# Point-cloud window attention inside a Perceiver/Mamba layer: points of a sub-block 15 apart, centre loads on another queue, and layer 2 with value matmuls of its own

## The reference, cut to what matters

```python
neigh = gather(feats, inds)                                  # one window of 10 neighbours per point and order
gf = concatenate([broadcast(center), neigh - center], -1)    # 2*C channels, stacked over the 4 orders
x16 = x.astype(float16).astype(float32)                      # (B*N, 10, 256), heads of 32 channels
scores = einsum('bihd,bjhd->bhij', qh, qh) / sqrt(32)        # 10 x 10 per point and head
attn = softmax(scores)
fused = einsum('bhij,bjhd->bihd', attn, qh) @ W_lin.T        # 64 outputs, folded with W_conv
# then instance norm, leaky relu, and the maximum over the 10 neighbours
```

## Time and profile before

| | |
|---|---|
| median of 3 runs | 2704.42 us (2703.09 to 2705.81) |
| the profiled execution, its own time | 2693.29 us |
| its span, first to last instruction | 2691.5 us |
| mean granted clock of PE | 0.87 of full speed |
| PE busy, share of the span | 1997.2 us, 74% |
| DVE busy | 1852.2 us, 69% |
| ACT busy | 1381.4 us, 51% |
| POOL busy | 778.7 us, 29% |
| DMA | 263.01 MB in 494619 packets, 98 GB/s |
| a pair's window loads | QW 240 KB, QX 3 x 80 KB and 240 KB |

### The profile page before, as it was taken

One profiled execution on the slowest core, in us unless ns is written; L12 is line 12 of the kernel. 1 busy time (PEld: TensorE's weight loads), 2 busy tenths in 40 slices (PEclk: granted clock), 3 DMA queues, 4 the chain that ended last, 5 costly groups with the idle time before them and its releaser, 6 DMA issues. The chain is left out here.

```text
span 2691.5 us, 119989 instructions
## 1 busy us (share of the span) xinstructions
PE 1997.2 (74%) x48106; PEld 1420.5 (53%) x48106; DVE 1852.2 (69%) x4073; ACT 1381.4 (51%) x2858; POOL 778.7 (29%) x996
## 2 busy tenths in 40 slices
PE   0586636666666656648888888885789999999977
PEld 0124325556555634338888888883334544454432
DVE  7889975555555559964555555557758888888875
ACT  0489843333333359834555555554564555555532
POOL 0010023443444420033333333330024444444321
PEclk9996667777778765678999999997999999999988
DMA  1105665555555516654555554542022222222210
GB/s 51 12 6 133 150 152 113 130 127 127 129 128 129 126 43 151 149 128 109 115 111 115 115 115 112 117 105 80 25 86 78 90 77 79 82 82 78 82 55 18
DMA packets 494619, 263.01 MB, mean 98 GB/s; under 512 B 362667, under 2 KB 463947, under 8 KB 494408
## 3 DMA queue, kind: packets, MB, share of 16 engines
q1 hardware_dynamic: 489512, 257.92, 39.8%
q10 hardware_dynamic: 5024, 4.00, 0.6%
HBM read 208.85 MB, written 52.96 MB: 97 GB/s over the span
## 5 line engine op out<-in xcount | busy, mean ns | idle before, releaser
L872 PE MATMUL pQ<-QW,QX 128*30 128x42 f16 (+1 forms) x23040 | 709.3, 298 | 297.6 <-DMA QX<-scratch_q 264.0
L872 PEld LDWEIGHTS pQ<-QW,QX 128*30 128x30 f16 x23040 | 659.7, 142 | 323.9 <-issue 322.2
L981 POOL TENSOR_TENSOR Ap<-E,RM 128x450 f32<-128x450 f32 x384 | 371.9, 969 | 59.7 <-POOL RM L976 58.6
L1011 ACT ACTIVATE E<-Dm 128x150 f32<-128x150 f32 x384 | 125.9, 328 | 465.7 <-DVE Dm L938 465.5
L955 DVE TENSOR_REDUCE hmax<-Hs 128x450 f32 (+1 forms) x144 | 89.7, 623 | 325.1 <-ACT junk L1023 325.1
L976 POOL TENSOR_TENSOR RM<-R,own 128x45 f32<-128x45 f32 x384 | 100.5, 262 | 671.4 <-DVE R L944 671.0
L1016 ACT ACTIVATE Vs<-pQ 128x480 f32<-128x480 f32 (+1 forms) x384 | 292.5, 762 | 0.0
L928 DVE TENSOR_REDUCE mx<-pQ 128x15 f32<-128x150 f32 x384 | 116.4, 303 | 218.9 <-PE pQ L872 217.8
L949 DVE STREAM_TRANSPOSE AT<-Ap 128x480 f32<-128x480 f32 x384 | 244.6, 637 | 21.1 <-POOL Ap L981 19.6
L1969 POOL TENSOR_TENSOR MT<-cb,decay 128x512 f32 (+1 forms) x128 | 163.9, 1302 | 244.8 <-PEq L1737 147.9
L609 DVE TENSOR_TENSOR QT<-ext,cen 128x1650 f16<-128x1650 f32 x96 | 233.0, 2488 | 1.8 <-issue 1.5
(11 more groups left out here) (365 smaller groups left out, 3295.1 us busy)
## 6 DMA issues: line engine op xcount, KB each, us to landing
QW<-scratch_q SPq DMA_DIRECT2D x192, 240.0 KB, 3.0
QX<-scratch_q SPq DMA_DIRECT2D x576, 80.0 KB, 2.6
QX<-scratch_q SPq DMA_DIRECT2D x192, 240.0 KB, 3.4
scratch_q<-QT SPq DMA_DIRECT2D x120, 360.0 KB, 5.0
Wg<-in_in_proj SPq DMA_DIRECT2D x64, 256.0 KB, 2.7
Wh<-in_in_proj SPq DMA_DIRECT2D x64, 256.0 KB, 2.8
Wo<-in_out_proj SPq DMA_DIRECT2D x64, 256.0 KB, 2.6
W_s<-in_in_proj SPq DMA_DIRECT2D x16, 256.0 KB, 2.7
```

Source lines behind the costliest of these rows:

```text
L872: last = nc.tensor.matmul(pQ[32 * h:32 * h + PTS * K, p, u // PB, at0:at0 + ON], query, both, start=True, stop=True)
L981: nc.gpsimd.tensor_tensor(subs(A[:, p, :], 32)[:, :, 0:PTS * K].rearrange("p s (n j) -> p s n j", n=PTS), subs(E[:, p, :], K).unsqueeze(2) ...
```

## The change

- Sub-blocks: the three points of a sub-block are now 15 apart, so that sub-block is the fastest index of the points. The subtractions read both operands in sequence: three of 1800, 1800 and 1500 elements, one of 30, one of 60. The centre matmuls and the maximum over neighbours follow the new order.
- Centre loads: one tile CT without slots, loaded for CU sub-tiles at a time (4 in layer 1, 2 in layer 2). In layer 1 ACT issues them, behind the copy of the values; in layer 2 SP issues them four steps later than before.
- Layer 2: the matmul of keys and weights becomes two. Scores use 96 rows and 10 key columns, values 128 rows and the 64 weight columns from their own contiguous tile; the four score matmuls of a sub-block come first, then the four value matmuls. PSUM is split into pS and pV. The weights are no longer copied into QW.
- Layer 2: the mix uses one matmul with 64 stationary columns where there were two with 32.
- The rest of CT is zeroed on DVE, the pad sub-blocks of QT cover two runs more, and the second result tile is allocated after the second gathering.

```diff
@@ -605,18 +604,17 @@
-                    for n in range(PTS):
-                        v.tensor_tensor(QT[:, k, 0:LAST, n, :, 0:SUBS],
-                                        rows(ext, k, ahead + n, (GP, LAST), (1, K), (PTS, SUBS)),
-                                        rows(cen, k, n, (GP, LAST), (0, K), (PTS, SUBS)),
+                    runs_of = QT[:, k, :, :, :, :].rearrange("p g n j u -> p (g n) j u")
+                    for r0, r1 in zip(THIRDS, THIRDS[1:]):
+                        v.tensor_tensor(runs_of[:, r0:r1, :, 0:SUBS],
+                                        rows(ext, k, ahead + SUBS * r0, (SUBS, r1 - r0), (1, K), (1, SUBS)),
+                                        rows(cen, k, SUBS * r0, (SUBS, r1 - r0), (0, K), (1, SUBS)),
                                         ALU.subtract).then_inc(q_v, 1)
...
@@ -749,8 +749,8 @@
-        QW = sb("QW", [128, NU, UT * 4, ON * SW], F16)
-        CT = sb("CT", [128, NU, UT * GP], F16)
+        QW = sb("QW", [128, NU, UT * 4, (ON if WIDE else K) * SW], F16)
+        CT = sb("CT", [128, U * GP], F16)
...
-        pQ = ps("pQ", [128, 2, NB, 512])
+        if WIDE:
+            pQ = ps("pQ", [128, 2, NB, 512])
+        else:
+            pS, pV = ps("pS", [128, 2, 512]), ps("pV", [128, 2, 1024])
...
+        def load_centres(eng, at, k):
+
+            (t, r), w = at, k // CU
+            c16 = scratch["c16"].rearrange("p (v x) -> p v x", x=CU * GP)
+            eng.wait_ge(mixed, pack(r, k + CU - 1) + 1)
+            eng.dma_start(CT[0:2 * C, w * CU * GP:(w + 1) * CU * GP],
+                          c16[:, bass.ds(r * (U // CU) + w, 1), :].rearrange("p v x -> p (v x)")).then_inc(c_in[w], 16)
@@ -836,11 +854,8 @@
-                    if first:
-                        sp.wait_ge(ct_zeroed, 1)
-                    sp.wait_ge(mixed, pack(r, k + UT - 1) + 1)
-                    sp.dma_start(CT[0:2 * C, w, :], c16[:, bass.ds(r * NU + w, 1), :].rearrange("p v x -> p (v x)"))\
-                        .then_inc(c_in[w], 16)
+                if at(4) and (k - 4) % CU == 0 and not WIDE:
+                    load_centres(sp, at(4), (k - 4) % U)
@@ -850,27 +865,40 @@
...
                         for h in range(4):
-                            y = k % UT * 4 + h
-                            query = QX[:, w, y, :, :].rearrange("p n (j u) -> p u (n j)", u=SW)[:, u]
-                            both = QW[:, w, y, :].rearrange("p (x u) -> p u x", u=SW)[:, u]
-                            at0 = u % PB * ON
-                            last = nc.tensor.matmul(pQ[32 * h:32 * h + PTS * K, p, u // PB, at0:at0 + ON], query, both,
-                                                    start=True, stop=True)
+                            to = slice(32 * h, 32 * h + PTS * K)
+                            if WIDE:
+                                last = nc.tensor.matmul(pQ[to, p, u // PB, at0:at0 + ON], query[h], keys[h],
+                                                        start=True, stop=True)
+                            else:
+                                nc.tensor.matmul(pS[to, p, u * K:u * K + K], query[h][0:96], keys[h][0:96],
+                                                 start=True, stop=True)
+                        if not WIDE:
+                            for h in range(4):
+                                to = slice(32 * h, 32 * h + PTS * K)
+                                last = nc.tensor.matmul(pV[to, p, u * O:u * O + O], query[h], W["stack"][:, h, :],
+                                                        start=True, stop=True)
@@ -879,25 +907,24 @@
...
                     for u in range(SUBS):
-                        for slot, half in strips:
-                            at0 = slot * O + 32 * half
-                            last = nc.tensor.matmul(pH[at0:at0 + 32, p, 32 * u:32 * u + PTS * K],
-                                                    Vs[:, (first + slot) % RV, u * O + 32 * half:u * O + 32 * half + 32],
+                        for slot in range(SL):
+                            last = nc.tensor.matmul(pH[slot * O:slot * O + O, p, 32 * u:32 * u + PTS * K],
+                                                    Vs[:, (first + slot) % RV, u * O:u * O + O],
...
@@ -913,10 +940,11 @@
-            for k in range(1, U, 3):
+            for k in range(1, U if WIDE else 0, 3):
                 v.tensor_copy(*weights_of(k)).then_inc(placed[k // UT], 1)
+            v.memset(CT[2 * C:, :], 0.0).then_inc(ct_zeroed, 1)
@@ -952,8 +980,9 @@
-                    v.tensor_reduce(hmax[:, bass.ds(q * GP, GP)],
-                                    Hs[:, p, :].rearrange("p (n j) -> p n j", j=K), X, ALU.max).then_inc(hmax_done, 1)
+                    v.tensor_reduce(hmax[:, bass.ds(q * GP, GP)].rearrange("p (n s) -> p s n", n=PTS),
+                                    Hs[:, p, :].rearrange("p (s n j) -> p s n j", n=PTS, j=K), X, ALU.max)\
+                        .then_inc(hmax_done, 1)
@@ -1013,8 +1041,10 @@
...
+                if at(1) and (k - 1) % CU == 0 and WIDE:
+                    load_centres(act, at(1), (k - 1) % U)
```

More of the change, by code:

```diff
@@ L774, in window_attention @@
         q_in = [sem(f"q_in{k}") for k in range(NU)]
-        c_in = [sem(f"c_in{k}") for k in range(NU)]
+        c_in = [sem(f"c_in{k}") for k in range(U // CU)]
         projected = sem("projected")
@@ L852, in _ @@
             none = A[:, 0:2, :].rearrange("p k x -> p (k x)").bitcast(F16)
[L853 to L856, removed]
+            if WIDE:
+                cells = [pQ[:, p, b, :] for p in range(2) for b in range(NB)]
+                pe.wait_ge(rows_zeroed, 1)
+            else:
+                cells = [pS[:, p, :] for p in range(2)] + [pV[:, p, 512 * b:512 * b + 512] for p in range(2) for b in range(2)]
+            for cell in cells:
+                nc.tensor.matmul(cell, none[:, 0:128], none[:, 0:512], start=True, stop=True)
             def scores(k, at):
@@ L881, in mix @@
                     pe.wait_ge(copied, q + 1)
-                    for w in range(first // UT, k3 // UT + 1):
-                        pe.wait_ge(c_in[w], r * 16 + 16)
-                    strips = [(slot, half) for slot in range(SL) for half in range(O // 32)]
-                    for slot, half in strips:
-                        at0 = slot * O + 32 * half
[L888 to L893, removed]
+                    pe.wait_ge(c_in[first // CU], r * 16 + 16)
+                    if isinstance(t, int):
+                        pe.wait_ge(ct_zeroed, 1)
+                    for slot in range(SL):
+                        for half in range(O // 32):
+                            at0 = slot * O + 32 * half
+                            out = pH[at0:at0 + 32, p, 0:GC].rearrange("p (s x) -> p s x", x=32)[:, :, 0:PTS * K]\
+                                .rearrange("p s (n j) -> p s n j", n=PTS)
+                            ctr = CT[:, (first + slot) * GP:(first + slot + 1) * GP].rearrange("p (n s) -> p s n", n=PTS)\
+                                .unsqueeze(3).to_broadcast([128, SUBS, PTS, K])
+                            nc.tensor.matmul(out, W["center"][:, 32 * half:32 * half + 32], ctr, start=True, stop=False)
                     pe.wait_ge(vs_ready, t + 3)
@@ L990, in _ @@
             act.dma_start(own[:, :], io["own"]).then_inc(const_in, 16)
-            for k in range(0, U, 3):
+            for k in range(0, U if WIDE else 0, 3):
                 nc.scalar.activation(*weights_of(k), ACT.Copy).then_inc(placed[k // UT], 1)
```

56 lines of the change are left out of this document (33 added, 23 removed).

## The result

The changed kernel takes 3022.64 us (median of 4 runs, 3016.68 to 3027.27), the kernel before 2703.76 us beside it: a ratio of 1.1187, 95% interval 1.115 to 1.1223, 319 us slower where 316 us faster was forecast. The profiled execution spans 3025.5 us against 2691.5, at a mean granted clock of 0.725 against 0.87.

What follows compares the result with a forecast made beforehand. It took waits to hold the attention layers, window loads queued behind SP's centre load, and nearly full DVE and ACT the gather. Gains of 136 + 147 + 26 + 7 = 316 us took 2704.4 to 2388 us; range 2300 to 2545.

Steps and rivals of the forecast that it cites:

- Centre loads, layer 1: Layer 1: moving centre loads to ACT ends SP's queue stall; 11.70 to 8.8 us per pack, 136 us gained.
- rival 4: Layer 1: the centre wait isn't what holds it, its beat stays; 2524 us in total, chance 0.04.
- Rival 1: Layer 1: window transfers at 150 GB/s replace the stall; 9.7 us per pack, 2430 us in total, chance 0.08.
- Gathering: Gather stage: longer sequential subtractions shorten DVE until ACT takes over; 0.8 us per step, 26 us gained.
- Scores and values: Layer 2: sixty matmuls per sub-tile become 120 faster ones; 1.35 us per sub-tile against 2.26.
- The block of 1.35 us: Layer 2: one sub-tile's separate score and value matmuls on PE, at 10.2 and 12 ns each.
- The wide mix of 0.96 us: Layer 2: mix with 64-column strips, 16 ns per half-pass, against 1.25 us; costed at nothing overall.
- The form of the beat: Layer 2: values ready 1.93 us after the mix, then block and mix; 5.0 us per pack, 147 us gained.
- 2: Layer 2: a matmul with its weight load can't beat 23.6 ns; 2587 us in total, chance 0.12.
- 3: Layer 2: alternating 96 and 128 rows empties the array at each change; about 2849 us, chance 0.06.
- Start of layer 2: Between the layers: no stacked weights copied in, so PE's wait for them goes; 7 us gained.

Runs made afterwards that it cites:

- Experiment 13: experiment 1 with the centre loads back on SP at their earlier place, two sub-tiles each, in both layers: 2673.8 us.
- experiment 8: experiment 2 with scores and values separate in the second sub-tile of each pack of layer 2: 2506.9 us.
- experiment 9: experiment 2 with scores and values separate in five of the six sub-tiles of layer 2's loop, 1704 instructions: 2728.4 us.
- experiment 12: The changed kernel with each wide mix matmul of layer 2 cut to 32 of 64 weight columns, same instruction count: 2947.7 us.
- experiment 6: experiment 2 with scores (96 rows) and values separate in the first sub-tile of each pack of layer 2: 2540.3 us.
- experiment 2: experiment 1 with layer 2's mix in one strip of 64 columns instead of two of 32: 2538.6 us.
- experiment 7: experiment 6 with the separate scores taken over all 128 rows instead of 96: 2536.8 us.
- experiment 1: The changed kernel with layer 2's scores and values merged again and its mix in 32-column strips: 2479.95 us in five rounds, ratio 0.9211 to the kernel before.
- experiment 14: experiment 1 with 22 of the 45 sub-blocks of second sub-tiles split into scores and values, 1640 instructions: 2463.88 us, ratio 0.9148 to the kernel before.
- experiment 3: experiment 2 with 60 repeated one-column score matmuls added per sub-tile of layer 2, as many matmuls as the changed kernel: 2995.4 us.

## Why the prediction was wrong

The profiled spans differ by 334 us. Up to the first read-out of layer 1 the change gains 15; in layer 1's packs 549.9 became 430.6 (-119); between the layers -10; in layer 2's packs 622.3 became 1088.8 (+466); behind them +12, which nothing here explains.

- *Centre loads, layer 1*: right. Forecast 8.8 us per pack, measured 9.16; 119 us instead of 136, inside the ends. Experiment 13 shows it to be this wait (rival 4 falls). Rival 1 falls too: the loads run at the 165 GB/s that the forecast took, not at 150, and PE no longer waits for them. What makes it 9.16 and not 8.8 is open; the clock was 0.84 there, not near its upper level as foreseen.
- *Gathering*: right. First to last step, L616 now and L618 before:

```profile
L616 DVE TENSOR_TENSOR QT<-ext,cen x16: 256/260/266, 207.2 to 353.4; 128x60 f16<-128x60 f32 x16
```

```profile
L618 DVE TENSOR_TENSOR QT<-ext,cen x16: 221/222/224, 210.0 to 369.7; 128x60 f16<-128x60 f32 x16
```

  (369.7 - 210.0) / 15 = 10.65 and (353.4 - 207.2) / 15 = 9.75: 0.9 us per step against 0.8. Its large subtractions, by form:

```profile
L609 DVE TENSOR_TENSOR QT<-ext,cen 128x1800 f16<-128x1800 f32 x64 | 127.4, 2033 | 27.2 <-ACT ext L698 22.7 <-issue 4.5
L609 DVE TENSOR_TENSOR QT<-ext,cen 128x1500 f16<-128x1500 f32 x32 | 54.9, 1717 | 0.0
```

  2033 ns for 1800 elements, as foreseen, and DVE now waits for ACT.
- *Scores and values*: the step that failed. "Sixty matmuls per sub-tile become 120" was costed as time on the array and never as length of the loop; what a longer loop costs was no term and no rival. It comes to 11.46 - 6.13 = 5.3 us per pack (experiment 8 and the turns without fetches of experiment 9 give the 6.13), 95 x 5.3 = some 500 us. Of the 5.3, PE's idle time is 3.57 (experiment 12), and 1.5 is the mix at the low clock that came with the stops (3.42 us against 1.94).
- Under it lie two mis-sized terms. The block of 1.35 us took 1.83: 15 ns per matmul, at a clock of 1.00 (experiment 6) as at 0.50 (the changed kernel, between its stops), where I had taken 10.2 and 12. The wide mix of 0.96 us took 1.94: I had scaled the 68 ns of the earlier trace rows by the moving columns, 128 to 30, but the strips stayed 64 wide and two side by side, and that counts as well (experiment 2). Without fetches the beat would be 2.0 + 1.83 + 0.36 (centre) + 1.94 = 6.13 us, a gain of 40 us in layer 2 and not of 147. By this estimate the kernel without fetches takes 2520 to 2530 us, inside my range, but with most of layer 2's gain missing. The form of the beat was right: 2 us after the mix, a block, a mix. Two of its sums are slightly off, without weight for the result: 1.93 + 1.35 + 1.45 is 4.73 and not 4.8, and a block of 60 at 10.2 and 60 at 33 ns is 2.59 us, not 2.83.
- *Rivals*: 2 falls, at 15 ns and not 23.6, though it was right that short matmuls don't reach the pace of the mix; 3, the only one on the slower side, comes nearest (2849) by a mechanism that isn't there: experiments 6 and 7 are 3 us apart where it wanted 140. No rival had the loop's length in it.
- *Start of layer 2*: nothing gained. From the last gather step (1165.9 before, 1015.0 after) to the first read-out it is 35.3 us before, 41.3 after, and 35.7 with the merged form (experiment 1). The unrolled start has 300 more matmuls to run through, and this straight code outruns its fetching too. From 1030 to 1056 us six pieces are fetched and PE stands for "issue" for 9.2 us in five stops; in experiment 1, from 1028 to 1048 us, it is 0.6 us and three pieces. The first of them:

```profile
1036.50 0.24 PE L895 MATMUL pS<-QW,QX 96*30 96x10 f16 x3 [2.64 <-issue]
```


The kernel that keeps what helps is experiment 1, 215 us under the kernel before, or experiment 14, 231 under it.

## What to carry to other kernels

Count the instructions of a loop's body per engine, weight loads included, before splitting a matmul in two: here a body of 1644 ran from what was loaded, one of 1704 was fetched again on every second or third turn as a rule and one of 1824 on every turn. A turn with fetches took 32 to 36 us instead of 17 to 22, which outweighed every gain that the longer body brought. Where a body starts, against the pieces of 16 KB, was not varied, so the limit may lie a little elsewhere for another kernel. In a profile the signs are idle time put down to "issue" in the middle of a block, and more packets on the instruction queue than the straight code needs. Where two stages of a beat are unequal, shorten the block that nothing covers: the same edit gave nothing on the first block of a pack and 33 us on the second.

## What the runs showed of the hardware

- PE's loop: no repeated fetching at 1644 matmuls and weight loads, on every second or third turn as a rule at 1704, on all at 1824. The Trainium skill (Runtime: NRT & Kernel Launch, Instruction fetch mechanics) has PE's instruction store as 2048 instructions, refilled in blocks of 16 KiB (256 instructions) by the sequencer's own queue, with a taken branch out of the current window of two pages as a stall. The block size and the queue agree with the trace (5.29 MB in 323 packets). The limit doesn't: by 2048 the changed kernel's loop would have stayed loaded, by a window of two pages not even the loop of 1464, and the runs put the limit between 1644 and 1704, plus the waits and branches that are not counted here.
- A piece of 16 KB came every 3.7 to 3.9 us while the loop was fetched, though its packet took some 1.3 us (experiment 9). What fills the rest is open.
- The low granted clock came with the stops: 0.97 to 1.00 in layer 2 in the kernels without repeated fetching, 0.50 in the changed kernel, 0.61 and 0.80 in experiments 12 and 3, 0.97 and 0.60 in two neighbouring turns of the same loop, where it fell inside the first stop (experiment 9).
- Fp32 strips of 64 weight columns, two side by side, went at 32 ns per half-pass at the full clock and 57 at half (3.42 us for 60), strips of 32, four side by side, at 10 ns at the full clock. Matmuls of 30 strided weight columns with 10 strided or 64 adjacent moving columns took 15 ns at either clock, four heads side by side.
